# Graph attention sums: slots of 128 edges accumulated in PSUM in place of pairs of chunks added in SBUF by VectorE

## The reference

```python
def gat_conv(x, W, attn_l, attn_r, src, dst, n_nodes):
    H, D = attn_l.shape
    feat = (x @ W).reshape(n_nodes, H, D)
    el = jnp.einsum('nhd,hd->nh', feat, attn_l)
    er = jnp.einsum('nhd,hd->nh', feat, attn_r)
    e = jax.nn.leaky_relu(el[src] + er[dst], NEG_SLOPE)
    m = jax.ops.segment_max(e, dst, num_segments=n_nodes)
    ex = jnp.exp(e - m[dst])
    denom = jax.ops.segment_sum(ex, dst, num_segments=n_nodes)
    alpha = ex / denom[dst]
    out = jax.ops.segment_sum(alpha[:, :, None] * feat[src], dst, num_segments=n_nodes)
    return out.reshape(n_nodes, H * D)
```

## Time and profile before

| | |
|---|---|
| median of three runs | 3418.46 us |
| profiled execution, its own time | 3424.56 us |
| its span, first to last instruction | 3422.8 us |
| mean granted TensorE clock | 0.933 of full speed |
| PE busy | 2659.2 us (78%) |
| DVE busy | 2337.8 us (68%) |
| ACT busy | 1240.5 us (36%) |
| POOL busy | 1089.1 us (32%) |
| head loop, first multiplication to last addition | 1790.6 to 2905.6 us |

### The profile page before, as it was taken

How to read it: one execution, slowest core, us unless ns; L and a number is a source line. 1 busy time by engine, 2 the same in 40 slices (tenths; PEclk the granted TensorE clock), 3 DMA queues, 4 the chain that set the end, 5 groups by cost and what they waited for, 6 DMA issues and landing times.

```text
span 3422.8 us, 53700 instructions
## 1 busy us (share of the span) xinstructions
PE 2659.2 (78%) x19026; PEld 2005.0 (59%) x19026; DVE 2337.8 (68%) x3395; ACT 1240.5 (36%) x2962; POOL 1089.1 (32%) x1238
## 2 busy tenths in 40 slices
PE   3666675988989999779918777777777777884999
PEld 1666665544545555679916555555555555683888
DVE  7999997687223444677788777676677776523886
ACT  1777776010001111100016555555555554402443
POOL 3000000011101222100037777777777776002000
PEclk9999988999999999889959999999999999856999
DMA  4334334523457774212137777777777776160553
GB/s 128 155 155 170 159 155 171 187 93 108 146 172 252 251 259 142 97 40 55 51 101 196 199 200 200 198 201 197 198 203 204 200 199 186 64 173 19 165 166 111
DMA packets 306388, 541.15 MB, mean 158 GB/s; under 512 B 105166, under 2 KB 208352, under 8 KB 305744
## 3 DMA queue, kind: packets, MB, share of 16 engines
q1 hardware_dynamic: 236976, 312.43, 27.9%
q0 software_dynamic: 69152, 225.28, 23.9%
HBM read 423.69 MB, written 115.11 MB: 157 GB/s over the span
## 4 chain that ended last, share of the span: by engine, by line
PE 65%; DVE 19%; issue 7%; ACT 5%; POOL 2%; DMA 2%; SPq 0%; POOLq 0%; DVEq 0%; ACTq 0%
PE ps L1369 24%; PE ps L1178 13%; PE ps L1357 8%; PE ps L1318 8%; DVE a L523 6%; DVE a L519 3%; DVE a L726 3%; PE ps L1316 3%; ACT oht L1066 2%; PE ps L1095 2%; DVE a L520 2%; ACT oh L1068 2%; PE ps L1147 2%; PE ps L1206 1%; PE ps L1149 1%
## 5 line engine op out<-in xcount | busy, mean ns | idle before, releaser
L1466 POOL DMA_INDIRECT a<-t,srci x502 | 533.9, 1063 | 520.2 <-DVE a L763 333.3
L1369 PE MATMUL ps<-a,oh 128*128 128x260 f32 x2008 | 500.0, 394 | 216.0 <-ACT oh L1068 106.1
L1178 PE MATMUL ps<-a 128*128 128x512 f32 x1200 | 575.4, 611 | 15.0 <-DMA a<-at_d 14.0
L1369 PEld LDWEIGHTS ps<-a,oh 128*128 128x128 f32 x2008 | 366.8, 192 | 348.8 <-issue 160.9
L1066 ACT ACTIVATE oht<-iota,ndl 128x128 f32<-128x128 f32 x830 | 333.3, 402 | 500.6 <-PE ps L1369 460.6
L924 DVE TENSOR_TENSOR a<-a,exb 128x520 f32<-128x520 f32 x502 | 330.0, 699 | 191.9 <-DMA a<-t,srci 187.3
L1147 PE MATMUL ps<-a 128*128 128x200 bf16 x1568 | 332.2, 270 | 163.1 <-DVE a L519 65.6
L1369 PE MATMUL ps<-wts,oh 128*128 128x260 f32 x1312 | 328.8, 396 | 116.5 <-ACT oh L1068 75.9
L1466 POOL DMA_INDIRECT wts<-t,srci x328 | 348.6, 1063 | 99.9 <-issue 99.3
L1318 PE MATMUL ps<-tbl,a 128*128 128x200 bf16 (+1 forms) x4692 | 372.2, 218 | 6.2 <-issue 6.0
L1369 PEld LDWEIGHTS ps<-wts,oh 128*128 128x128 f32 x1312 | 239.5, 192 | 204.9 <-ACT oh L1068 104.2
(11 more groups left out here) (259 smaller groups left out, 3873.0 us busy)
## 6 DMA issues: line engine op xcount, KB each, us to landing
a<-at_d SPq DMA_DIRECT2D x60, 1280.0 KB, 6.1
at_d<-a SPq DMA_DIRECT2D x49, 800.0 KB, 3.3
mt_d<-a SPq DMA_DIRECT2D x49, 800.0 KB, 4.9
a<-mt_d SPq DMA_DIRECT2D x30, 1280.0 KB, 6.1
a<-ot_d SPq DMA_DIRECT2D x98, 320.0 KB, 3.0
a<-trlo_d SPq DMA_DIRECT2D x49, 512.0 KB
ot_d<-a SPq DMA_DIRECT2D x49, 320.0 KB, 5.5
a<-t,srci POOLq DMA_INDIRECT x502, 3.8
```

The costliest lines, as they stand in the source:

```text
L1178: m = e.matmul(acc[f].rearrange("p (x d) -> p x d", x=8), X[:, hi, P * f:P * (f + 1)], a, start=(hi == 0), stop=False, skip_group_check=True)
L1369: t = e.matmul(pbig[s % 3][:, 512 * u:512 * u + 260], oh[:, so, k, :], hrows[2 * r + k][:, 260 * u:260 * (u + 1)], start=(k == 0), stop=(k ...
L1466: e.indirect_dma_start(out=hrows[2 * r + k], out_offset=None, in_=t2, in_offset=bass.IndirectOffsetOnAxis(ap=srci[:, k, s:s + 1], axis=0)) ...
```

## The change

In words:

- The unit is a slot of 128 consecutive edges within one block of destinations. There are NS1 = 781 + 25 = 806 slots, each with one gather, one `ex` DMA of 128 x 8, one multiplication and two matmuls. Row buffers stay 20 (NR = 20, one slot each), `exb` is 16 deep and is freed by `head_mul`.
- PE adds into PSUM: a block of destinations has one of four PSUM pairs, at an address from a register (`hbank`), with `start=False`. All eight banks are zeroed first by matmuls with zeros. Registers are loaded once for 8 slots.
- ACT takes a block's pair out into `acc1` when its last slot is done (`hend`) and writes zeros into the pair; 25 times. ACT's Abs and Relu, DVE's `add_heads` and the clearing of `acc1` by DVE and POOL are gone.
- DVE makes the one-hots, 8 slots at a time, in one `is_equal` of 128 x 1024 (`places`), 3 groups deep.
- The 16 sweeps that spread the carried maximum become 16 `scalar_tensor_tensor` (add, max) with masks `firstm` and `lastm`. Two scans in `CONV1` make the masks.
- The preparing jobs move: `gather rows` with 7 indirect DMAs to step 101, `rows to float` to 106, `table` to 108 to 111, `slots` to 112.

```diff
@@ jobs of CONV1
-        123: ["gather rows2"], 127: ["rf2 src"], 130: ["rf2 dst"], 134: ["slots2"]}
+        101: ["gather rows"], 106: ["rows to float"], 112: ["slots"]}
...
+for i_ in range(4):
+    JOBS.setdefault(108 + i_, []).append(("table", i_))
@@ vector, job "neg"
+                        e.tensor_tensor_scan(firstm[:, 0:J], negh[:, :], negh[:, :], 0.0, ALU.add, ALU.min).then_inc(*V.inc())
+                        e.tensor_tensor_scan(lastm[:, 0:J][:, ::-1], negt[:, ::-1], negt[:, ::-1], 0.0, ALU.add, ALU.min).then_inc(*V.inc("row ends"))
@@ vector, attention
-                for h in range(H):
-                    sweep(fv, fv, negh, h, cin[:, 0, h:h + 1])
-                e.wait_ge(*V.last())
-                for h in range(H):
-                    sweep(fv, fv, negt, h, cin[:, 1, h:h + 1], True)
+                for m, w in ((firstm, 0), (lastm, 1)):
+                    for h in range(H):
+                        e.scalar_tensor_tensor(out=fv[:, :, h], in0=m[:, 0:J], scalar=cin[:, w, h:h + 1], in1=fv[:, :, h],
+                                               op0=ALU.add, op1=ALU.max).then_inc(*V.inc())
@@ vector, head loop
-            e.memset(acc1[:, 0:6400], 0.0).then_inc(*V.inc("acc clear"))
...
-                for k in range(2):
-                    bv = hrows[2 * r + k].rearrange("p (h d) -> p h d", h=8)
-                    e.tensor_tensor(bv, bv, col(exb[:, s % 8, 8 * k:8 * k + 8], 65), ALU.mult).then_inc(head_mul, 1)
-                if s >= 2:
-                    add_heads(s - 2)
+            def places(g):
+                n = min(OG, NS1 - OG * g)
+                if g >= OHR:
+                    e.wait_ge(head_mm, OG * (g - OHR + 1))
+                e.tensor_tensor(ohs[g % OHR][:, 0:n, :], every(iota[:, :], n), col(dl1[:, OG * g:OG * g + n], P), ALU.is_equal).then_inc(head_oh, 1)
+
+            places(0)
+            for s in range(NS1):
+                if s % OG == 0 and s + OG < NS1:
+                    places(s // OG + 1)
+                r = s % NR
+                e.wait_ge(gh_in[r], 16 * (s // NR + 1))
+                e.wait_ge(ex_in[s % 16], 16 * (s // 16 + 1))
+                bv = hrows[r].rearrange("p (h d) -> p h d", h=8)
+                e.tensor_tensor(bv, bv, col(exb[:, s % 16, :], 65), ALU.mult).then_inc(head_mul, 1)
@@ scalar
+            for b in range(NB):
...
+                pair = ps[:, 1024 * (b % 4):1024 * (b % 4 + 1)].rearrange("p (u w) -> p u w", u=2)[:, :, 0:260]
+                e.wait_ge(head_mm, e.snap(hreg[b % 4], min_val=1, max_val=NS1))
+                e.activation(acc1[:, W1 * b:W1 * (b + 1)].rearrange("p (u w) -> p u w", u=2), pair, ACT.Copy).then_inc(head_out, 1)
+                e.wait_ge(head_out, b + 1)
+                e.activation(pair, bc(mzero[:, :].rearrange("p (a b) -> p a b", a=1), [P, 2, 260]), ACT.Copy).then_inc(acc_free, 1)
@@ tensor
+            for s in range(NS1):
+                r = s % NR
+                if s % OG == 0:
+                    k = s // P
+                    e.load(hbreg, hbank[k:k + 1, s % P:s % P + OG])
+                    e.load(hfreg, hfree[k:k + 1, s % P // 2:s % P // 2 + 4])
+                    e.wait_ge(head_oh, s // OG + 1)
+                if s % 2 == 0:
+                    e.wait_ge(acc_free, e.snap(hfreg[s % OG // 2], min_val=1, max_val=NB))
+                e.wait_ge(head_mul, s + 1)
+                o = ps[:, bass.ds(e.snap(hbreg[s % OG], min_val=0, max_val=3 * 1024), 1024)].rearrange("p (u w) -> p u w", u=2)
                 for u in range(2):
+                    t = e.matmul(o[:, u, 0:260], ohs[s // OG % OHR][:, s % OG, :], hrows[r][:, 260 * u:260 * (u + 1)], start=False, stop=True,
+                                 skip_group_check=True)
@@ gpsimd
-            for s in range(NR):
-                gather_heads(s)
-            e.wait_ge(*V("leaky", 8))
-            e.memset(acc1[:, 6400:], 0.0).then_inc(pool_clear, 1)
...
+            for s in range(NS1):
                 r = s % NR
                 if s >= NR:
                     e.wait_ge(head_mm, s - NR + 1)
+                e.indirect_dma_start(out=hrows[r], out_offset=None, in_=t2,
+                                     in_offset=bass.IndirectOffsetOnAxis(ap=src1[:, s:s + 1], axis=0)).then_inc(gh_in[r], 16)
```

More of the change, by code:

```diff
@@ L33 @@
 GRP = 5
-NR = 10
+NR = 20
+OG = 8
+OHR = 3
 W1 = 520
@@ L341, in program @@
         gh_in = [sem(f"gh_in{r}") for r in range(NR)]
-        ex_in = [sem(f"ex_in{q}") for q in range(8)]
+        ex_in = [sem(f"ex_in{q}") for q in range(16)]
         out_done = sem("out_done")
@@ L610, in job @@
                     e.tensor_copy(smalli[:, 0:NB], mp[1][:, 0:NB]).then_inc(*V.inc("counted"))
-                    plan(8, 4, NC, 336, 67, "plan2")
+                    e.memset(hend[:, :], NS1).then_inc(*V.inc())
+                    plan(7, 7, N1, 304, 60, "plan")
+                    e.tensor_copy(hend[:, 0:NB - 1], small[0:1, 65:64 + NB]).then_inc(*V.inc("block ends"))
+                elif kind == "rows to float":
+                    e.wait_ge(rows_in, 16 * 7)
+                    e.tensor_copy(rsf.rearrange("p (k w) -> p k w", k=7), rows[:, :, 0:P]).then_inc(*V.inc("rsf"))
+                    for k in range(7):
+                        e.tensor_scalar(rdf[:, P * k:P * (k + 1)], rows[:, k, P:2 * P], small[:, 320 + k:321 + k], None, ALU.add).then_inc(*V.inc("rdf"))
+                elif kind == "table":
+                    tab, (k0, k1) = (src1, dl1)[name[1] // 2], ((0, 4), (4, 7))[name[1] % 2]
+                    e.wait_ge(pe_prep, PREP[name])
+                    e.tensor_copy(tab[:, P * k0:P * k1], mp[1][:, 0:P * (k1 - k0)]).then_inc(*V.inc(name))
+                elif kind == "slots":
+                    e.wait_ge(pe_prep, PREP["slots"])
+                    e.tensor_copy(br1[:, :], mp[1][0:7, 0:P]).then_inc(*V.inc())
+                    e.tensor_scalar(hfree[:, :], mp[1][0:7, 1:P:2], 1.0, None, ALU.add).then_inc(*V.inc())
+                    e.tensor_copy(hchunk[:, :], mp[1][0:7, P:2 * P]).then_inc(*V.inc("slots"))
+                    e.wait_ge(*V.last())
+                    e.tensor_scalar(hbank[:, :], br1[:, :], 3, 10, ALU.bitwise_and, ALU.arith_shift_left).then_inc(*V.inc("slot banks"))
+                    e.memset(trb[0][:, 6, :], 0.0).then_inc(*V.inc())
+                    e.memset(trb[1][:, 6, :], 0.0).then_inc(*V.inc())
                 elif kind == "turned":
```

185 lines of the change are left out of this document (65 added, 120 removed).

## The result

The changed kernel takes 3450.91 us (median of 4 runs, 3447.43 to 3453.49), the kernel before on the same chip 3418.08 us (4 runs, 3412.96 to 3421.23). The ratio is 1.0097 with a 95% interval of 1.0079 to 1.0114: the change makes the kernel slower by 1.0%, 32.8 us by the medians. The profiled execution took 3449.51 us, 24.95 us over that of before (which lay 6.5 us above its median); the traces have to explain those 25 us, and say nothing of the 7.9 us by which the medians differ more.

What follows compares the result with a forecast made beforehand. POOL's gather issue, delayed by DVE's SBUF operations, bounds the head loop. +22.3 - 13.5 - 2.7 - 1.7 + 2.5 = +6.9 us on 3418.46 gives 3425 us; own range 3402 to 3449, whole range 3363 to 3468.

Steps and rivals of the forecast that it cites:

- all three signs for the loop: Head loop: gathers 1.12 us on the mean, 0.30 between, over half above 0.96; DVE waits for gathers; PE waits about 0.3.
- The period, 785 x 1.43 = 1122.6 us: Head loop: 785 gather periods of 1.43 us against 1100.3 us before, +22.3 us.
- each comes alone, 3.83 us after its own gather's start: Head loop: multiplications, formerly in pairs of 1.31 us, come singly and can meet a gather each time.
- The same equation: Head loop: even delay d = 4.53 - 3.75 - 3d - 0.125, so d = 0.164 and a period of 1.41 us.
- The sweeps, -13.5 us: Maximum's sweeps: 16 operations of 0.91 us, 14.6 us in all, replace scans on the path; -13.5 us.
- if stride-8 columns cost double: Sweeps: the stated bound at which their gain would be 0 instead of -13.5 us.
- One-hots and multiplications: DVE in the head loop: 101 one-hots of 1.22 us each and 806 multiplications of 0.70 us.
- Start and end: Edges of the head loop: -2.7 us up to POOL's restart, -1.7 us from the last gather's start to `den`.
- Jobs, +2.5: Preparing work ahead of the sweeps: two more scans +2, later table gather +0.5; +2.5 us (-2 to +8).
- After the loop, nothing: From `den` to the end of the span: no change, 0 us.
- PE under 1.33 us a slot: Head loop: PE needs 1.0 us of records plus at most 0.33 of register loads, covered by the gather's 1.43.
- rival 3: Head loop: PE's register loads or longer blocking push the period past 1.50 us; 3496 us, chance 0.16.

Runs made afterwards that it cites:

- contig: Changed kernel with the 16 sweep operations over 782 adjacent columns instead of every eighth, giving wrong values; 3473.47 us, one run.
- before_again: The kernel before, unchanged, run again for a trace on another chip with a lower granted clock; 3500.42 us.
- operands_psum: Changed kernel with one input of each DVE loop operation in PSUM, exponentials copied there by PE; 3467.24 us, ratio 0.9908 to the kernel before.
- operands_again: The kernel of operands_psum run once more on a third chip; 3480.06 us, ratio 0.9897 to the kernel before.
- before_psum: The kernel before with its exponentials copied to PSUM by ACT, 8 steps at a time; 3504.57 us, ratio 1.0012 to the kernel before.
- iota_psum: Changed kernel with the one-hots' comparison row in PSUM and two PSUM pairs for four; 3477.4 us, ratio 0.9874 to the kernel before.
- operands_fill: The filler run: operands_again plus one unneeded 128 x 512 bf16 matmul a slot on PE; 3493.04 us, ratio 0.9931 to the kernel before.
- after_third: The changed kernel itself, unaltered, on a third chip; 3480.52 us, ratio 0.9899 to the kernel before.
- after: The changed kernel's profiled execution on the first chip; 3449.51 us (median of its 4 runs 3450.91 us).

## Why the prediction was right, and where its sizes were off

Right were the mechanism and the period within its bounds (1.4485 us, forecast 1.40 to 1.46). The direction was right by little: +6.9 us is what the forecast itself calls the edge of no change, and it gave 0.44 to slower and 0.40 to faster. The profile shows +24.95, and the median of 3450.91 us lies inside the whole range but 2 us past the 3402 to 3449 of the forecast's own. Some of it is the chip's doing: on two others the same change made the kernel faster. On the first chip all three signs for the loop came: gathers of 1.143 us on the mean (1.12 forecast), 72% of them over 0.96 us (40% before), 0.30 us between. DVE waits for gathers, and POOL never waits for PE once the loop runs. PE waits 0.3 to 0.5 us for most slots.

1. *The period, 785 x 1.43 = 1122.6 us.* Measured 1.4485, which is 14.5 us of the miss and its largest term. The step that was off is "each comes alone, 3.83 us after its own gather's start". That distance is of an undisturbed gather. Behind the first 30 gathers, multiplications follow the start of their gather by 3.89 us where the gather took under 0.96 us, and by 4.09 us where it took over 1.3; the mean is 4.01. A delayed gather also lands later, so its multiplication moves after the third gather instead of clearing it. The same equation with 4.01 gives d = (4.01 + 0.70 - 3.75 - 0.125) / 4 = 0.209 us and a period of 1.459. That is now too much, so an even delay for all is only a rough picture; the count gives the sizes. Sorted by the DVE operation in which they start, 656 of the 786 gathers start in a multiplication and lose 148.7 us, 15 in a one-hot and lose 7.0 us, and 115 in none and lose 0.1. So multiplications cost 0.189 us a gather (0.164 forecast), one-hots 0.009 (0.02). In the kernel before 434 of 810 started in a multiplication (89.3 us) and 272 in the addition L916, whose input is in PSUM, and lost 0.2 us. That is what the change took away: the addition gave DVE something to do that blocked nobody.
2. *The sweeps, -13.5 us.* Measured -3.3: L816 took 1.61 us, not 0.97. The bound was named ("if stride-8 columns cost double") and the value taken at the wrong end; `contig` shows 1.03 us for adjacent columns.
3. *One-hots and multiplications*: 1.218 and 0.701 us, as forecast (1.22, 0.70).
4. *Start and end*: -2.2 and -2.4 for -2.7 and -1.7. ACT's copy took 0.60 us.
5. *Jobs, +2.5*: all ahead of the sweeps came 1.0 us later. The stretch of CONV1 grew by 4.8, and the work on either side of it gave 3.8 back.
6. *After the loop, nothing*: -4.9, most of it in the second look-up stage (110.7 us before, 106.5 after). The kernel before itself took 513.0 us from `den` on in `before_again`, for 517.2 here, so this need not come of the change.
7. *PE under 1.33 us a slot*: four records took 1.14 us and the loop ran at 1.4485, so it was covered. The register loads were priced too high: they took 0.59 and 0.33 us for eight slots, 0.12 a slot for 0.33, and even that is hidden, since PE starts 0.25 us behind the end of a multiplication at the first slot of eight as at the others. On the three other chips PE decides part of the loop, as in rival 3, but neither at its period (1.476 and 1.486 us, not over 1.50) nor for its reason: the stops fall at any of a slot's four matmuls and not at the register loads alone. The prediction took PE's pace on one chip, with the granted clock of 0.99 of the earlier trace rows, as given for all.

The Trainium skill ("SBUF — State Buffer", section "Who interferes with whom") names two SBUF inputs as the condition for contending with a GpSimd instruction that reads SBUF. The runs agree: with one input in PSUM, mean gathers of 0.945 to 0.948 us in `operands_psum`, `operands_again` and `before_psum`. The remark in the same section that a probe saw `tensor_tensor` not stall a DMA does not hold for these gathers: the 656 that started in one lost 0.227 us each on the mean.

What stays open: the size of the gain on a chip like the first. If PE could follow, operands_psum would have 785 periods of at least 1.25 us against 1.4485, an estimate from gaps and undisturbed gathers. PE may well follow: eight of its records in a row take 1.99 us at full clock, 1.0 us for a slot's four, and the register loads add at most 0.12 us a slot, which makes 1.1 us, again an estimate. No run fell on such a chip, so this wasn't shown. Nor was the effect of pairing shown there. Of the candidates, `operands_psum` and `iota_psum` beat the kernel before on their chips (by 0.9 to 1.0% and 1.3%); that either beats the changed kernel was not seen.

## What to carry to other kernels

Where GpSimd's indirect DMAs set the pace, count not how long VectorE is busy but how many of them start while it runs an operation with two SBUF inputs, and let a delayed gather's landing move with it in the reckoning; one operand in PSUM takes the delay away, at the price of bringing it there. Taking non-blocking work off VectorE gains nothing there and can shift the blocking work into the way. Before trusting a per cent, look in both kernels at the granted clock of the stretch, and at how long after PE's matmuls the engines that wait for them start: the same change lost 1.0% on a chip where that was 0.04 us each time and won 0.9 to 1.0% on two where it was up to 11 us. A low clock is no proof that the clock is the cause: see which comes first, and whether a fuller clock helps.

## What the hardware showed beyond that

- The same program got a granted clock of 0.99 in the head loop on one chip and 0.88 on another, and took 3418 and 3500 us; in the two profiles the part from the first multiplication to `den` took 1115.0 and 1198.9 us, and all the rest 8 us less on the second. The stretches at the lower level sum to 17 us of the loop's 1100 on the first chip and 263 on the other. The Trainium skill ("TensorE: Matmul & The Clock Gate", section "Loop structure matters more than you think") makes the clock a matter of the loop nest. The filler run agrees with that (0.88 to 0.97), but the same loop with 0.99 and 0.88 on two chips doesn't follow from it.
- PE can stand still for 0.3 to 2.4 us before a matmul that waits for nothing, and do so at full clock: 111 of 156 such stops in `after_third`, 198 of 200 in `operands_fill`, none in `after`.
- An fp32 `scalar_tensor_tensor` over 782 columns takes 1.03 us with adjacent columns and 1.61 us with a step of 32 bytes.
- A gather of 128 rows of 2080 bytes costs POOL 0.945 us where nothing delays it, plus 0.305 us between two, on all four chips.
